# Three graph-attention layers on one core: new set-up of the score columns, new load order, new cyclic issue order

## The reference

```python
# x (32, 256, 256) f32, adj (32, 256, 256) int32 (about 1/16 ones); each of the 32 batches is independent
def layer_A(h, adj, W, a):                      # one head
    Wh = h @ W
    e = leaky_relu(Wh @ a[:256] + (Wh @ a[256:]).T, 0.2);  e = where(adj == 0, -1e9, e)
    return elu(softmax(e, axis=2) @ Wh)
def gat(x, mask, W, a_src, a_dst, bias):        # B: 4 heads of 128; C: 1 head of 256
    xl = x @ W
    e = leaky_relu(asrc[s] + adst[d], 0.2);  e = where(mask, e, -1e9)
    return softmax over s, weighted sum of xl, + bias
mask = (adj > 0) | eye
x = layernorm(x + layer_A(x, adj, ...))
x = layernorm(x + gat_C(elu(gat_B(x, mask, ...)), mask, ...))
```

## Time and profile before

| | |
|---|---|
| runs | 669.05 us median of 3 (668.47 to 672.19) |
| profiled execution | 667.11 us, of which the span from first to last instruction is 665.2 us |
| PE busy | 637.9 us (96%) |
| DVE busy | 588.7 us (88%) |
| ACT, POOL busy | 482.0 us (72%), 448.6 us (67%) |

### The profile page before, as it was taken

One profiled execution on the slowest core, in us unless ns is written; L12 is line 12 of the kernel. 1 busy time (PEld: TensorE's weight loads), 2 busy tenths in 40 slices (PEclk: granted clock), 3 DMA queues, 4 the chain that ended last, 5 costly groups with the idle time before them and its releaser, 6 DMA issues. The chain is left out here.

```text
span 665.2 us, 17485 instructions
## 1 busy us (share of the span) xinstructions
PE 637.9 (96%) x4156; PEld 574.9 (86%) x4156; DVE 588.7 (88%) x2315; ACT 482.0 (72%) x1220; POOL 448.6 (67%) x811
## 2 busy tenths in 40 slices
PE   6979999999999999999999999999999999999993
PEld 5758899998999999999999989999999999988871
DVE  1488999999999999999999999999999999899953
ACT  1457887787778777777787777778877777687661
POOL 0247577777777777677777777777777777666762
PEclk9999999999999999999999999999999999999996
DMA  8311112222212222221122222211222222210001
GB/s 269 96 48 36 46 49 80 81 65 81 67 37 75 81 81 80 65 81 62 40 77 81 81 67 78 81 48 50 80 81 80 65 80 73 89 33 0 18 17 47
DMA packets 46693, 45.68 MB, mean 69 GB/s; under 512 B 2817, under 2 KB 46337, under 8 KB 46594
## 3 DMA queue, kind: packets, MB, share of 16 engines
q1 hardware_dynamic: 45648, 43.79, 20.8%
q10 hardware_dynamic: 946, 0.80, 0.4%
HBM read 36.19 MB, written 8.39 MB: 67 GB/s over the span
## 5 line engine op out<-in xcount | busy, mean ns | idle before, releaser
L378 POOL TENSOR_SCALAR probB<-probB,rdenB 128x256 f32<-128x256 f32 x256 | 124.7, 499 | 79.9 <-DVE rdenB L958 79.6
L558 ACT ACTIVATE probB<-probB,shiftB 128x256 f32<-128x256 f32 x256 | 127.1, 499 | 16.8 <-DVE shiftB L927 13.0
L1524 PE MATMUL PS<-probTB,VB 128*128 128x256 f32 x512 | 128.2, 382 | 0.9 <-ACT probTB L577 0.8
L941 DVE SCALAR_TENSOR_TENSOR probB<-PS,VB,gatedB 128x256 f32<-128x256 f32 x256 | 111.5, 478 | 1.8 <-issue 0.4
L389 POOL TENSOR_TENSOR inlC<-hidT,inhC 128x512 fp32r<-128x512 f32 x64 | 82.0, 1281 | 43.7 <-ACT inhC L622 43.6
L899 DVE CUSTOM_DVE_ANT_0 gatedB<-PS,gate_bc 128x256 f32<-128x256 f32 x256 | 93.8, 420 | 7.3 <-PE PS L1494 5.5
L1524 PEld LDWEIGHTS PS<-probTB,VB 128*128 128x128 f32 x512 | 89.3, 190 | 11.0 <-ACT probTB L577 2.1
L1480 PE MATMUL PS<-WhB,inhB 128*128 128x260 f32 x256 | 81.8, 319 | 1.4 <-DVE inlB L972 1.2
L577 ACT ACTIVATE probTB<-PS 128x512 f32<-128x512 f32 x128 | 72.9, 591 | 9.9 <-PE PS L1505 9.6
L360 POOL TENSOR_TENSOR y<-y,xres 128x512 f32<-128x512 f32 x32 | 41.1, 1286 | 52.4 <-DVE y L963 52.4
L1480 PE MATMUL PS<-WhC,inhC 128*128 128x258 f32 x256 | 75.4, 294 | 0.5 <-issue 0.4
(11 more groups left out here) (108 smaller groups left out, 1626.1 us busy)
## 6 DMA issues: line engine op xcount, KB each, us to landing
adj_in<-in_adj_dram SPq DMA_DIRECT2D x32, 256.0 KB, 4.3
xTin<-in_x_t_dram SPq DMA_DIRECT2D x32, 256.0 KB, 4.1
adjT_in<-in_adj_t_dram SPq DMA_DIRECT2D x32, 256.0 KB, 3.1
xres<-in_x_dram SPq DMA_DIRECT2D x32, 256.0 KB, 2.8
out_dram<-res SPq DMA_DIRECT2D x32, 256.0 KB, 2.1
WTC<-in_L_gnn_W_t_dram SPq DMA_DIRECT2D x1, 512.0 KB, 7.4
WTB<-in_L_gnn_W_t_dram ACTq DMA_DIRECT2D x1, 512.0 KB, 8.0
WB<-in_L_gnn_W_dram SPq DMA_DIRECT2D x2, 256.0 KB, 8.3
```

What stands on the lines that cost most here:

```text
L378: last = pool.tensor_scalar(B.prob[h][:, k, :], B.prob[h][:, k, :], B.rden[:, k, h:h + 1], 1.0, ALU.mult, ALU.mult)
L558: last = nc.scalar.activation(L.prob[h][:, k, :], L.prob[h][:, k, :], ACT.Exp, bias=L.shift[:, k, h:h + 1], accum_out=den[:, k, h:h + 1] i ...
L941: last = nc.vector.scalar_tensor_tensor(out=L.prob[h][:, k, :], in0=PS[b][:, (h % 2) * N:(h % 2 + 1) * N], scalar=L.V[:, k, h, 1:2], in1=L ...
L1524: last = nc.tensor.matmul(PS[b][:, o:o + N], B.V[:, k, h, 2:B.F + 2], B.probT[h][:, k, :], start=(k == 0), stop=(k == NT - 1))
```

## The change

1. **Score columns.** `score_products`, the transposed weights and the packed vectors are gone. The attention vectors are loaded as rows repeated over all 128 partitions, and DVE multiplies W by them and sums along the row, 28 instructions in all: 4 for A and 8 for C of 256 elements, 16 for B of 128.
2. **Loads.** SP issues A's weights and the first xT, then waits until A's weights have landed before it issues anything else; ACT likewise after A's vectors. ACT and PE no longer wait for the identity at their start (`spread` does, for batch 0).
3. **Ones multiplied in TensorE's gaps.** `warm_up(b, n)` issues n f32 matmuls of a 128x128 tile of ones. Before: 4 at the start. Now 11 at the start, 10 more in the fill, and 12 in the drain between the last `spread` and the last `transpose_weights`.
4. **Body.** All lists in `body(i)` have a new cyclic order and new banks. Some steps are only counted to another turn (`low_c`, `scale(2)`, `diagonal`, `load_residual`).
5. **Fill and drain** are written anew on every engine, in the same style, to fit.

```diff
+        def load_vectors(eng, L):
+            if L is A:
+                eng.dma_start(A.att[:, :, :], a0.rearrange("(j f) o -> j (f o)", j=2).partition_broadcast(P))\
+                    .then_inc(A.s_attld, DMA)
+            else:
+                for j, v in enumerate((asrc1, adst1) if L is B else (asrc2, adst2)):
+                    eng.dma_start(L.att[:, j, :], v.rearrange("h f -> (h f)").partition_broadcast(P))\
+                        .then_inc(L.s_attld, DMA)
...
# SP, fill
                 load_weights(sp, A)
+                load_xT(b0)
+                sp.wait_ge(A.s_wld, DMA)
                 load_adj(b0)
-                load_xT(b0)
                 load_xT(b1)
-                load_weights_T(sp, C)
+                load_weights(sp, C)
+                load_xT(b2)
                 load_weights(sp, B)
                 load_adj(b1)
                 load_adjT(b0)
+                load_xT(b3)
                 load_residual(b0)
...
# ACT, fill
-                load_weights_T(act, A)
-                load_vectors(act)
+                load_vectors(act, A)
+                act.wait_ge(A.s_wld, DMA)
+                load_biases(act)
+                load_vectors(act, C)
+                load_vectors(act, B)
                 load_table()
...
# DVE
+            def score_columns(L, k, heads):
+                dve.wait_ge(L.s_wld, (B.KT if L is B else 1) * DMA)
+                dve.wait_ge(L.s_attld, (1 if L is A else 2) * DMA)
+                for h in heads:
+                    for j in range(2):
+                        v = L.att[:, 1 - j if L is A else j, h * L.F:(h + 1) * L.F]
+                        if L.columns > 1:
+                            dve.wait_ge(L.s_wab, L.columns - 1)
+                        nc.vector.scalar_tensor_tensor(out=L.prod[:, j, :], in0=L.W[:, k, h, 2:L.F + 2],
+                                                       scalar=0.8 if j == 0 else -0.8, in1=v, op0=ALU.mult, op1=ALU.mult,
+                                                       accum_out=L.W[:, k, h, j:j + 1]).then_inc(L.s_wab, 1)
+                        L.columns += 1
...
# DVE, fill (new): A's columns first, then
+                score_columns(A, 0, (0,))
+                score_columns(A, 1, (0,))
                 make_gate_a(b0)
+                maxima(A, 0, 6, b0)
...
+                shift(A, 0, b0)
+                score_columns(C, 0, (0,))
+                score_columns(C, 3, (0,))
+                score_columns(C, 1, (0,))
+                score_columns(C, 2, (0,))
+                score_columns(B, 1, (0, 1))
+                inverse_sum(A, 0, 5, b0)
                 make_gate_a(b1)
+                inverse_sum(A, 1, 4, b0)
                 make_gate_b(b0)
+                split_weights(C)
                 elu_first(b0)
+                score_columns(B, 1, (2, 3))
+                score_columns(B, 0, (0, 1))
+                stats(A, b0)
+                meanvar(A, b0)
                 maxima(A, 0, 6, b1)
+                score_columns(B, 0, (2, 3))
+                logit(A, 0, 6, b1)
...
# PE, body (new order)
+                project(B, 0, 1, 3, t3)
+                project(B, 1, 1, 7, t3)
+                transpose_weights(B, 1, 0, t4)
+                transpose_weights(A, 0, 2, t2)
+                spread(B, 1, 6, t3)
+                transpose_weights(C, 0, 1, t5)
+                weigh_head(1, 4, t4)
+                weigh(A, 1, 0, t2)
+                project(B, 1, 0, 3, t3)
+                project(B, 0, 0, 5, t3)
+                weigh(A, 0, 1, t2)
+                spread(B, 0, 3, t3)
+                weigh(C, 1, 4, t5)
+                weigh(C, 0, 0, t5)
+                project_a(0, 2, t1)
+                project_a(1, 1, t1)
+                transpose_weights(B, 2, 6, t3)
+                project(C, 0, 0, 7, t4)
+                project(C, 1, 0, 2, t4)
+                transpose_weights(B, 3, 1, t3)
+                spread(A, 0, 6, t1)
+                spread(C, 0, 0, t4)
+                weigh_head(2, 5, t3)
+                transpose_weights(B, 0, 3, t3)
+                transpose_x1(7, t2)
+                weigh_head(3, 5, t3)
+                weigh_head(0, 4, t3)
...
# PE, end of drain
+                spread(C, 0, 4, e1)
+                warm_up(7, 12)
+                transpose_weights(C, 0, 2, e1)
+                weigh(C, 1, 7, e1)
+                weigh(C, 0, 4, e1)
```

More of the change, by code:

```diff
@@ L47, in last, with gat_kernel @@
         return self.at * step
-def gat_kernel(nc, x, xT, adj, adjT, w0, w0T, w1, w1T, w2, w2T, vectors, biases, out):
+def gat_kernel(nc, x, xT, adj, adjT, w0, a0, w1, asrc1, adst1, w2, asrc2, adst2, biases, out):
     NB, N, D = x.shape
@@ L667, in fill @@
-                values(A, 1, 5, b3)
+                exp(B, 3, b0)
+                norm_first(1, 6, b1)
+                norm_first(0, 1, b1)
+                elu_exp_first(b1)
+                weights_copy(B, 2, 7, b0)
+                exp(B, 0, b0)
+                values(A, 0, 3, b2)
+                values(A, 1, 2, b2)
+                weights_copy(B, 3, 0, b0)
+                exp(B, 1, b0)
+                weights_copy(B, 0, 0, b0)
+                elu_exp(1, 1, b0)
+                high_b(4, b1)
@@ L1289, in drain @@
                 maxima(B, 0, 2, e3)
+                logit(B, 0, 2, e3)
+                top(B, 0, e3)
+                elu_first(e2)
+                shift(B, 0, e3)
                 inverse_sum_head(3, e3)
-                inverse_sum(C, 0, 0, e5)
-                logit(B, 0, 2, e3)
-                maxima(A, 0, 5, e1)
+                logit(B, 1, 2, e3)
+                inverse_sum(C, 1, 1, e5)
+                stats(A, e2)
                 meanvar(A, e2)
-                inverse_sum(C, 1, 1, e5)
@@ new lines, in drain @@
+                inverse_sum(C, 0, 5, e4)
+                norm_last(1, 1, e4)
+                maxima(C, 0, 7, e3)
+                norm_last(0, 5, e4)
+                logit(C, 0, 7, e3)
+                inverse_sum_head(1, e2)
+                stats(C, e4)
+                meanvar(C, e4)
+                top(C, 0, e3)
+                low_b(0, e1)
+                shift(C, 0, e3)
+                elu(1, 1, e2)
+                values_b(1, 1, 0, e1)
+                values_b(0, 1, 6, e1)
+                maxima(B, 3, 6, e1)
@@ new lines, in fill @@
+                project_a(0, 1, b1)
+                project_a(1, 6, b1)
+                transpose_weights(A, 0, 4, b0)
+                weigh(A, 0, 5, b0)
+                weigh(A, 1, 4, b0)
+                project_a(1, 2, b2)
+                project_a(0, 3, b2)
+                spread(A, 0, 6, b1)
+                column_sums(0)
+                spread_b1(7)
+                transpose_x1(4, b0)
+                warm_up(1, 2)
+                project(B, 0, 1, 6, b0)
+                project(B, 1, 1, 5, b0)
@@ L1585, in fill @@
+                weigh_head(3, 1, b0)
+                weigh_head(0, 0, b0)
+                transpose_x1(4, b1)
+                project(B, 0, 1, 4, b1)
+                project(B, 1, 1, 3, b1)
+                transpose_weights(B, 1, 4, b0)
+                spread(B, 1, 6, b1)
+                transpose_weights(A, 0, 1, b2)
+                weigh_head(1, 0, b0)
+                project(B, 1, 0, 2, b1)
                 project(B, 0, 0, 3, b1)
+                weigh(A, 1, 7, b2)
+                spread(B, 0, 1, b1)
@@ L1613, in fill @@
[L1613 to L1625 removed]
+                transpose_weights(B, 2, 6, b2)
@@ new lines, in drain @@
+                project(B, 0, 0, 3, e4)
+                weigh(A, 1, 0, e3)
+                weigh(A, 0, 6, e3)
+                spread(B, 0, 7, e4)
+                weigh(C, 1, 1, e6)
+                project_a(0, 2, e2)
+                weigh(C, 0, 4, e6)
+                project_a(1, 0, e2)
+                project(C, 1, 0, 5, e5)
+                project(C, 0, 0, 3, e5)
+                transpose_weights(B, 2, 7, e4)
+                spread(A, 0, 4, e2)
+                transpose_weights(B, 0, 6, e4)
```

1255 lines of the change are left out of this document (558 added, 697 removed).

## The result

The changed kernel takes 667.35 us (median of 7 runs, 666.89 to 668.44) against 669.35 for the kernel before beside it (7 runs, 668.47 to 672.19): ratio 0.9968, interval 0.9952 to 0.9983. The forecast was -5.0 us; the chip gave -2.0. The two profiled executions point the other way (668.44 after, 667.11 before), because the one of before was faster than every timed run and the one of after was the slowest of its seven. So a difference of two profiles is read here by its parts, each checked on other executions, and not by its sum.

A forecast was written before the change was run, and what follows sets the result against it. PE bounds the saturated body, with a dependency loop in each 19.12 us turn, plus a late head and cold tail. Head -5.5, body +2.5, tail -2.0 sum to -5.0: 669.05 to 664.0 us, range 658.5 to 670.5.

The forecast's parts named there:

- rival 2: Whole kernel: gain swallowed, head -3, body +3.5, tail -2, sum -1.5, 667.5 us; chance 0.28 shared with other small sums.
- I carry 5.5 us to the body: Head: earlier chains let the body begin 5.5 us earlier, bounds 2 and 8.
- a gain that is gone when the body begins: Sign of error: head's gain lost by the body's first transpose_x1, at 105.84 before.
- A's operands at 3.6 to 4.6: Head: A's vectors land at 3.6 to 4.6 us, bounds 3.6 to 6; first projection at about 6.3.
- `maxima` near 9: Head: batch 0's maxima moves from 14.86 to 9.2 us if the clock is up, 5.6 earlier.
- `norm_first` near 16: Head: norm_first starts near 16 us, 6.3 earlier than 22.33, after C's last column at 14.5.
- body "+2.5": Body: about 0.1 us more a turn over 25 turns, +2.5 us; bounds 0 and +6.
- The stalls I named: Body: high_b 0.05 us later, spread(C) 0.03 to 0.08 late, weigh(A, 1) 0.02 to 0.05 late, each turn.
- Rival 3's sign: Body: DVE idle before maxima(A) each turn; its rival had turns 0.45 us longer, 672.8 us, chance 0.12.
- ones at the end, -2.0: Drain: 12 ones matmuls in PE's 3.24 us gap hold the clock, saving 2.0 us.
- drain "lose about as much; 0", at most 1.2: Drain: new order can win at most PE's 1.2 us idle from 583.7 to 640, or lose as much; taken 0.
- the two cases weighed: Head: clock up, two projections take about 1.8 us, maxima 5.6 earlier; or still cold, 3.6 earlier.

The follow-up runs named there:

- e2: Changed kernel's body and drain with the fill of the kernel before on every engine: 668.44 us, ratio 1.0000.
- e7: Changed kernel without the two waits of the load queues for A's weights: 664.99 us, ratio 0.9950.
- e10: e7 with 28 more ones multiplications ahead of the first x1 transposes and 16 more behind them: 663.21 us, ratio 0.9922.
- e5: Kernel before plus 12 ones multiplications, in free bank 1, between the last spread and the last weight transposes: 666.11 us, ratio 0.9975.
- e14: e12 with first residual load and two loads behind it ahead of the fourth batch's xT, and 10 ones instead of 28: 664.46 us, ratio 0.9923.
- e16: e14 with 11 ones instead of 4 at the start and 12 more ahead of the first weight transposes: 660.62 us, ratio 0.9857.
- e6: Changed kernel without its 12 ones ahead of the last weight transposes: 669.04 us, ratio 1.0008.
- e3: Changed kernel's fill and body with the drain of the kernel before plus ones in bank 7: 671.84 us, ratio 1.0035.
- e1: Kernel before plus 12 ones multiplications, in held bank 7, between the last spread and the last weight transposes: 671.29 us, ratio 1.0029.
- e8: Changed kernel with B's first two score columns moved behind elu_first and the other eight behind meanvar: 668.31 us, ratio 0.9995.
- e9b: Profile of: order of before in all stages, new score columns and loads, no holds, 12 end ones in bank 1; timed 669.43 us, ratio 0.9996.
- e12: The kernel of e9b with 28 more ones ahead of the first x1 transposes and 20 behind: 667.59 us, ratio 0.9971.

## Why the prediction was wrong

The total came near rival 2's (-1.5), but not by its terms: it had the body at +3.5 and the end at -2, where the runs show 0 and +0.8 (3.1 less the 2.3 of the ones).

**Failed: "I carry 5.5 us to the body".** This term of the sum was mis-sized. The new fill brings 1 to 2 us by e2, and the sign that I had named, a gain that is gone when the body begins, did show: the body's first `transpose_x1` came at 106.45, before at 105.84. Four steps of the chain were off, and the yardstick too:
- *A's operands at 3.6 to 4.6.* They came at 5.5, within the bounds, and the first projection started at 7.10, not 6.3. I took the 2.8 of the earlier trace rows as the price of an uncrowded load; A's weights took 4.7 to 4.9 beside the repeated vectors, with or without holds. The columns themselves were cheaper than I took them: 0.35 us from one to the next, not 0.42.
- *`maxima` near 9.* It came at 11.03: the projections' end was followed by the ACT table load, which the hold had kept back to 8.34, and only then by the copies.
- *`norm_first` near 16.* I checked C's columns against the path and let B's ride along at 1.1 us without asking when WB lands. It landed at 18.7, and `inverse_sum(A)` was queued behind. I also costed the holds at nothing. Taking both holds away brought `norm_first` to 16.86 and the ratio from 0.9968 to 0.9950.
- *The clock.* I weighed it for the first projection alone. The early head opened gaps for PE (3.17 us before 22.29), and the first `project(B)` ran at half clock: 2.5 us from T0 to T4 by e7 and e10. It is tempting to say that the work which the change took off PE had been cover for the clock; that isn't shown, for in e2 and e5 the clock fell with that work in place.
- *The yardstick.* I measured the gain from one profile of before, at 105.84 the earliest of the four that have the old fill (up to 110.23 in e5). That was luck of the draw, and it flatters the old head.

What is earlier at T0 does reach the end: e7, e10, e14 and e16 keep it to within some tenths. So apart from the clock the first turns swallow nothing.

**Failed: body "+2.5".** It is 0. The stalls I named exist, but a loop takes the sum of its links: 0.05 more ahead of `high_b` was given back threefold ahead of `low_b` (means of 24 turns: 0.77 to 0.62). And though the loop got 0.1 us shorter in the mean, the turn stayed 19.12: this loop alone does not set the turn. I had added the losses of three waits and none of their slack. Rival 3's sign is there and harmless: DVE waits 0.44 us before `maxima(A)` in each of 24 turns, and PE doesn't wait for it.

**Right: ones at the end, -2.0.** Measured 1.9 (e5) and 2.3 (e6), through the two rows named.

**Failed: drain "lose about as much; 0", at most 1.2.** T28 to the end is 3.1 us longer without the ones (e6). My bound took only 583.7 to 640 of before. What was lost is the place of the last `spread(C)`, 652.60 after and 649.16 before, whose timeline has it just ahead of the last transposes of the earlier trace rows:

```profile
649.16 0.40 PE L1494 MATMUL PS<-ident,VC 128*128 128x128 f32 x2 [0.57 <-ACT VC L548]
```

The distance from T28 to this `spread` grew from 84.4 to 87.25 us, and with PE doing the same 532 records in it PE's idle time grew from 3.1 to 5.3. Six waits of 0.25 us and more between 621 and 641, where before has none, sum to 2.5; three are for `scale` on POOL, one each for `weights_copy` and `low_b`, and one has no releaser in the profile. Two of them:

```profile
621.49 0.63 PE L1502 MATMUL PS<-ident,probB 128*128 128x128 f32 x4 [0.46 <-POOL probB L381]
...
626.55 0.36 PE L1475 MATMUL PS<-WhB,inhB 128*128 128x260 f32 x1 [0.67 <-DVE inlB L975]
```

e2, with the old fill, has the same six. Whether the new list of the drain opens these waits or the phase in which the new body hands over to it stays open. e3 can't tell: its last `spread` lies as far from T28 (87.2), but by other waits, those of its seam.

**The sum.** With ones at -2.3 and the end at +3.1, a total of -2.0 asks for a head of -2.8; e6 (0.9 above before, +3.1 at the end) asks for -2.2, e2 for 1 to 2. So the head's term stays open between -1 and -3. The profiles can't settle it, since the head of before itself varies by over 4 us: the four profiles with the old fill and no ones added in it (before, e1, e2, e5) give T0 from 31.12 to 34.77 and, at batch 4, 105.84 to 110.23. Their mean at batch 4, 108.2, is 2.0 later than that of the changed kernel, e3 and e6 (106.2), in the middle of that range.

On the clock at the start, the prediction weighed a rule (the Trainium skill, TensorE: Matmul & The Clock Gate, What's actually happening: how many matmuls run cold varies from run to run). The traces agree in small: with 11 ones ahead the first projection took 1.98 us in nine of ten traces and 2.29 in the tenth (e8), with 4 ones 3.54 to 3.78. So of the two cases weighed the warm one came each time.

## What to carry to other kernels

When the work ahead of a dependent chain comes earlier, look for the gaps that open in TensorE: its clock may fall in them, and a few multiplications of ones ahead of the fall, in a bank that nothing holds, are worth microseconds, while behind the fall or in a held bank they cost as much. In a queue that works in order, every wait (a hold, a column that needs a late load, a load that needs a free buffer) is a wait of all that stands behind it, so list those before costing it at nothing. Before you measure a gain from one profile, see how much the same stretch varies between executions. An issue order belongs to the orders of the other engines: parts of two schedules joined need their loads checked anew.

## What the runs showed of the hardware

- A load of one row repeated over 128 partitions (256 KB in SBUF) took 4.2 us, and the plain 256 KB load beside it 4.7 where it had taken 2.8.
- One VectorE multiply with a running sum took 0.29 us with 0.21 from one to the next for 128 elements. While POOL added the residual, one took 1.34:

```profile
22.51 1.39 POOL L363 TENSOR_TENSOR y<-y,xres 128x512 f32<-128x512 f32 x1 [20.60 <-DVE y L966]
...
22.71 1.34 DVE L851 SCALAR_TENSOR_TENSOR prodB<-WB,attB 128x128 f32<-128x128 f32 x1
```

The Trainium skill (GPSIMD Engine Reference, the table's row on SBUF interfaces) says that VectorE instructions with two SBUF inputs contend with GpSimd for shared interfaces; this instruction has two, and the row agrees. e9b agrees from the other side: there the residual was added only at 26.00, and the multiply in the same place (third behind `elu_first`) took

```profile
23.00 0.29 DVE L849 SCALAR_TENSOR_TENSOR prodB<-WB,attB 128x128 f32<-128x128 f32 x1
```

Twelve traces have the residual beside that multiply, and it takes 1.34 to 1.35 in each; e9b and e12 have them apart, and it takes 0.29. That the shared interface is the cause was not tried by itself.
